# Softmax maxima of an attention kernel: split ahead of the turn, and the diagonal blocks' decay and maximum in one instruction

## The reference

```python
q, k, v = x @ W_q, x @ W_k, x @ W_v              # x is layer-normed
latent_kv = (k + v) @ W_down_kv
k_rec, v_rec = latent_kv @ W_up_k, latent_kv @ W_up_v   # 16 heads of 16
scores = einsum('bhqd,bhkd->bhqk', qh, k_rec) / math.sqrt(d)
scores = scores * exp(-0.01 * abs(t[:, None] - t[None, :]))
attn = softmax(scores)
out = (attn @ v_rec) @ W_o
x = x + out
```

## Time and profile before

| | |
|---|---|
| median of 3 runs | 6739.2 us (6736.05 to 6740.18) |
| profiled execution | 6737.1 us |
| its span on the core | 6735.3 us |
| PE busy | 5578.3 us (83%) |
| DVE busy | 4789.2 us (71%) |
| ACT busy | 3487.3 us (52%) |
| POOL busy | 2918.9 us (43%) |
| granted TensorE clock, mean | 0.919 |

### The profile page before, as it was taken

How to read it: one execution, slowest core, us unless ns; L and a number is a source line. 1 busy time by engine, 2 the same in 40 slices (tenths; PEclk the granted TensorE clock), 3 DMA queues, 4 the chain that set the end, 5 groups by cost and what they waited for, 6 DMA issues and landing times.

```text
span 6735.3 us, 109029 instructions
## 1 busy us (share of the span) xinstructions
PE 5578.3 (83%) x35596; PEld 3237.8 (48%) x35596; DVE 4789.2 (71%) x10653; ACT 3487.3 (52%) x5077; POOL 2918.9 (43%) x2244
## 2 busy tenths in 40 slices
PE   5489993688888889889888898898889975499992
PEld 5478882233433344334333443343434445388872
DVE  7655552677877878778778788787787867555674
ACT  1134442366666666666666666666666651144431
POOL 6700004455445454554555555545545117600166
PEclk9999996799999999999999999999999985599996
DMA  5433332333333333333333333333333225333486
GB/s 175 160 99 105 105 104 84 89 96 94 101 96 95 96 99 94 94 97 99 94 96 92 102 96 89 103 93 94 99 91 94 71 68 184 143 101 104 134 262 217
DMA packets 573334, 741.96 MB, mean 110 GB/s; under 512 B 104434, under 2 KB 490612, under 8 KB 572788
## 3 DMA queue, kind: packets, MB, share of 16 engines
q1 hardware_dynamic: 523636, 600.70, 30.4%
q0 software_dynamic: 49152, 134.28, 6.1%
HBM read 441.30 MB, written 293.34 MB: 109 GB/s over the span
## 4 chain that ended last, share of the span: by engine, by line
PE 57%; DVE 16%; POOL 15%; issue 7%; ACT 4%; DMA 1%; SPq 0%; POOLq 0%; DVEq 0%; ACTq 0%
PE psum L1059 11%; PE psum L346 10%; PE psum L948 9%; PE psum L958 7%; POOL xs L617 7%; PE psum L363 5%; DVE at_mx L1187 4%; DVE at_Sd L1183 2%; POOL at_qs L1267 2%; DVE at_mp L1208 2%; PE psum L961 2%; DVE at_mp L1210 2%; PE psum L1037 2%; DVE at_mab L1191 2%; PE psum L335 2%
## 5 line engine op out<-in xcount | busy, mean ns | idle before, releaser
L1187 DVE TENSOR_REDUCE at_mx<-psum 128x4 f32<-128x512 f32 x3584 | 2224.1, 681 | 704.3 <-PE psum L948 704.2
L1131 ACT ACTIVATE at_P<-psum 128x1024 f32<-128x1024 f32 x2048 | 2036.1, 1021 | 867.6 <-PE psum L961 865.7
L948 PE MATMUL psum<-at_kst,at_qst 96*128 96x128 bf16 (+3 forms) x7168 | 1350.7, 298 | 402.7 <-DVE at_mx L1187 384.5
L948 PEld LDWEIGHTS psum<-at_kst,at_qst 96*128 96x128 bf16 x7168 | 557.2, 99 | 1344.2 <-DVE at_mx L1187 844.8
L958 PE MATMUL psum<-at_qst,at_kst 99*128 99x512 bf16 (+3 forms) x5120 | 1153.3, 324 | 29.7 <-ACT at_P L1131 27.7
L1059 PE MATMUL psum<-at_P,at_V 128*17 128x512 f32 x8192 | 1125.1, 622 | 0.0
L1279 POOL TENSOR_TENSOR at_Sd<-at_Sd,at_m 128x1024 f32<-128x1024 f32 x256 | 484.7, 1906 | 527.3 <-DVE at_m L1201 524.0
L958 PEld LDWEIGHTS psum<-at_qst,at_kst 99*128 99x128 bf16 x5120 | 478.5, 100 | 311.9 <-ACT at_P L1131 49.0
L1230 POOL DMA_INDIRECT at_xT<-ys,at_yib x256 | 245.7, 960 | 790.8 <-DMA at_gab<-table 709.4
L961 PE MATMUL psum<-at_ident,at_Sd 128*128 128x128 f32 x2048 | 572.9, 280 | 0.0
L1258 POOL TENSOR_TENSOR at_OT<-at_On,at_rc 128x128 f32<-128x128 f32 x256 | 98.3, 405 | 1004.2 <-DVE at_rc L1215 1004.2
(11 more groups left out here) (248 smaller groups left out, 8214.2 us busy)
## 6 DMA issues: line engine op xcount, KB each, us to landing
parts<-at_pt SPq DMA_DIRECT2D x768, 128.0 KB
at_qst<-parts SPq DMA_DIRECT2D x1536, 64.0 KB, 2.3
at_kst<-parts SPq DMA_DIRECT2D x256, 192.0 KB, 3.0
m2X<-xs SPq DMA_DIRECT2D x272, 128.0 KB, 2.0
ys<-m2X SPq DMA_DIRECT2D x272, 128.0 KB
m1X<-xs SPq DMA_DIRECT2D x264, 128.0 KB, 2.0
ys<-m1X SPq DMA_DIRECT2D x264, 128.0 KB
at_kst<-parts SPq DMA_DIRECT2D x256, 128.0 KB, 2.9
```

Source lines behind the costliest of these rows:

```text
L948: ins = e.matmul(bank[(z + u) % 3][:, col - 512 * u:col - 512 * u + ln], self.qst[0:96, s, side, 128 * t:128 * t + 128], self.kst[0:96, s, ...
L1131: e.activation(self.P[:, i % NP, :], slot[a % 2], ACT.Exp).then_inc(self.taken.sem, 1)
L1187: e.tensor_reduce(self.mx[:, p % 2, hh, 8 * o + 4 * u:8 * o + 4 * u + 4], of, op=ALU.max, axis=AX.X).then_inc(self.s_read.sem, 1)
```

## The change

"mlo" and "fold" are gone from the plan. In the item "max", DVE now splits the maxima where they are, with queries on partitions: cast, subtract, cast, subtract on 128 x 16, into `mb` (128 x 3 x 16, bf16). PE turns all three parts with one bf16 matmul against a bf16 identity (48 rows out), after waiting for `m_parts`. ACT changes the sign in one copy of 48 x 128, and SP stores that, in another order of the DRAM tensor, so that each of the four loads reads rows of 1024 numbers. The diagonal blocks are read by `tensor_tensor_reduce`, one instruction for a block of 128 columns, which multiplies by `Dm`, writes `Sd` and gives the block's maximum.

```diff
--- before.py
+++ after.py
@@ -20,6 +20,7 @@
 E = 8
 B = 16
 LAM = 0.01
+LOWEST = -3.0e38
 EPS = 1e-5
 NBLK = 272
 XROWS = 16 * 128 * 89
@@ -675,7 +676,8 @@
         self.ve, self.sq, self.rs = sb("ve", [128, 8]), sb("sq", [128, 8]), sb("rs", [128, 8])
         self.mx, self.mab = sb("mx", [128, 2, 2, 56]), sb("mab", [128, 2, 16])
         self.m = sb("m", [128, 2, 16])
-        self.mT, self.mp = sb("mT", [16, 2, 128]), sb("mp", [16, 2, 3, 128], BF16)
+        self.mb, self.mr = sb("mb", [128, 2, 3, 16], BF16), sb("mr", [128, 16])
+        self.mp, self.identb = sb("mp", [48, 2, 128], BF16), sb("identb", [128, 128], BF16)
         self.yib, self.gab = sb("yib", [128, 8, 2], U32), sb("gab", [128, 8, 2])
         self.rows = self.xT[:].rearrange("p k (t d) -> p (k t) d", d=D)
         ctx.close()
@@ -698,6 +700,7 @@
         self.s_filled, self.s_read = sig.new("a_s_filled", 32 * NPAIR), sig.new("a_s_read", 32 * NPAIR)
         self.shifted = sig.new("a_shifted", 2 * NPAIR)
         self.m_max, self.m_parts = sig.new("a_m_max", NPAIR), sig.new("a_m_parts", NPAIR)
+        self.ident_cut = sig.new("a_ident_cut", 1)
         self.weighed, self.ou_copied, self.shared = sig.new("a_weighed", 8 * NPAIR), sig.new("a_ou_copied", NPAIR), sig.new("a_shared", NPAIR)
         self.spread, self.inverse = sig.new("a_spread", B), sig.new("a_inverse", NPAIR)
         self.summed = sig.new("a_summed", 4 * B)
@@ -708,7 +711,7 @@
         yield from (("weight", 0), ("weight", 1), ("weight", 2))
         yield from (i for f in (self.gather_order, self.prep_order) for i in f(0) if i)
         ahead = [i for b in range(1, B) for i in ((b, self.gather_order(b)), (b, self.prep_order(b)))]
-        late, after, split, fold = [], [], None, None
+        late, after, split = [], [], None
 
         def advance(queue):
             for item in queue[0][1]:
@@ -728,16 +731,10 @@
             score = (z // 8, self.ORDER[z % 8]) if z < 8 * NPAIR else None
             turn = (p, kb) if 0 <= s < 8 * NPAIR else None
             if split is not None:
-                yield from (("mlo", split), ("msend", split))
+                yield ("msend", split)
                 split = None
             if score or turn:
                 yield ("step", score, turn)
-            if fold is not None:
-                yield ("fold", fold, 1)
-                fold = None
-            if score and score[1] == self.DIAG:
-                yield ("fold", score[0], 0)
-                fold = score[0]
             if score and z % 8 == 7:
                 yield ("max", score[0])
                 yield ("sub", 2 * score[0] + 1)
@@ -911,13 +908,12 @@
             if kind == "msend":
                 p = at[0]
                 s, z = p % NS, p % 2
-                w.wait_ge(*self.m_parts.at(p + 1))
-                e.dma_start(self.mdram[z], self.mp[:, z]).then_inc(self.m_out.sem, 16)
+                w.wait_ge(*self.result("mturn", p))
+                e.dma_start(self.mdram[z].rearrange("c h t q -> (c h t) q"), self.mp[:, z]).then_inc(self.m_out.sem, 16)
                 w.wait_ge(*self.m_out.at(16 * (p + 1)))
                 for hh in (1, 0):
                     for v in range(2):
-                        e.dma_start(self.qst[96:99, 2 * s + hh, v, :].rearrange("c (t q) -> c t q", q=128),
-                                    self.mdram[z, 8 * hh:8 * hh + 8].rearrange("t c q -> c t q")).then_inc(self.m_rows[s].sem, 16)
+                        e.dma_start(self.qst[96:99, 2 * s + hh, v, :], self.mdram[z, :, hh].rearrange("c t q -> c (t q)")).then_inc(self.m_rows[s].sem, 16)
             if kind == "res":
                 b, t2 = at
                 w.wait_ge(*self.x1_out.at(16 * (b + 1)))
@@ -1013,8 +1009,9 @@
                 ins.then_inc(self.filled.sem, 1)
             if kind == "mturn":
                 p = at[0]
-                w.wait_ge(*self.m_max.at(p + 1))
-                e.transpose(to[0:16, 0:128], self.m[:, p % 2, :], self.ident[:]).then_inc(self.filled.sem, 1)
+                w.wait_ge(*self.m_parts.at(p + 1))
+                w.wait_ge(*self.ident_cut.at(1))
+                e.matmul(to[0:48, 0:128], self.mb[:, p % 2].rearrange("p c n -> p (c n)"), self.identb[:], start=True, stop=True).then_inc(self.filled.sem, 1)
             if kind == "norm":
                 p = at[0]
                 w.wait_ge(*self.ou_copied.at(p + 1))
@@ -1107,8 +1104,7 @@
             if kind == "mturn":
                 p = at[0]
                 w.wait_ge(*self.m_out.at(16 * (p - 1)))
-                e.activation(self.mp[:, p % 2, 0, :], of[0:16, 0:128], ACT.Copy, scale=-1.0)
-                e.activation(self.mT[:, p % 2, :], of[0:16, 0:128], ACT.Copy, scale=-1.0).then_inc(self.taken.sem, 1)
+                e.activation(self.mp[:, p % 2, :], of[0:48, 0:128], ACT.Copy, scale=-1.0).then_inc(self.taken.sem, 1)
             if kind == "norm":
                 p = at[0]
                 w.wait_ge(*self.shared.at(p - 1))
@@ -1145,6 +1141,7 @@
         w.wait_ge(*self.loaded.at(176))
         e.tensor_tensor(self.wk[:], self.wk[:], self.wv, ALU.add).then_inc(self.w_ready.sem, 1)
         e.tensor_scalar_mul(self.wq[:], self.wq[:], 1.0 / 16.0).then_inc(self.w_ready.sem, 1)
+        e.tensor_copy(self.identb[:], self.ident[:]).then_inc(self.ident_cut.sem, 1)
         last, z = None, 0
         for kind, *at in self.plan:
             if kind == "stats":
@@ -1180,34 +1177,31 @@
                         if o == self.DIAG:
                             if p >= 2:
                                 w.wait_ge(*self.full("T", p - 2, 7, hh))
-                            e.tensor_tensor(self.Sd[:, (2 * p + hh) % 4, 4 * u:4 * u + 4], of, self.Dm[:].rearrange("p (o k) -> p o k", o=1).to_broadcast([128, 4, 128]),
-                                            ALU.mult).then_inc(self.s_read.sem, 1)
+                            for t in range(4):
+                                ins = e.tensor_tensor_reduce(self.Sd[:, (2 * p + hh) % 4, 4 * u + t, :], of[:, t], self.Dm[:], 1.0, LOWEST, ALU.mult, ALU.max,
+                                                             accum_out=self.mab[:, 1, 8 * hh + 4 * u + t:8 * hh + 4 * u + t + 1])
+                            ins.then_inc(self.s_read.sem, 1)
                         else:
                             w.wait_ge(*self.m_max.at(p - 1))
                             e.tensor_reduce(self.mx[:, p % 2, hh, 8 * o + 4 * u:8 * o + 4 * u + 4], of, op=ALU.max, axis=AX.X).then_inc(self.s_read.sem, 1)
-            if kind == "fold":
-                p, hh = at
-                w.wait_ge(*self.s_read.at(32 * p + 4 * self.ORDER.index(self.DIAG) + 4))
-                last_fold = own.end(e.tensor_reduce(self.mab[:, 1, 8 * hh:8 * hh + 8], self.Sd[:, (2 * p + hh) % 4], op=ALU.max, axis=AX.X))
             if kind == "max":
                 p = at[0]
                 w.wait_ge(*self.s_read.at(z))
-                w.wait_ge(*last_fold)
                 k = own.end(e.tensor_reduce(self.mab[:, 0, :], self.mx[:, p % 2].rearrange("p h (t k) -> p (h t) k", k=7), op=ALU.max, axis=AX.X))
                 w.wait_ge(*k)
                 w.wait_ge(*self.shifted.at(2 * (p - 1)))
                 if p >= 2:
                     w.wait_ge(*self.full("mturn", p - 2))
                 e.tensor_tensor(self.m[:, p % 2, :], self.mab[:, 0, :], self.mab[:, 1, :], ALU.max).then_inc(self.m_max.sem, 1)
-            if kind == "mlo":
-                p = at[0]
-                mT, mp = self.mT[:, p % 2], self.mp[:, p % 2]
-                w.wait_ge(*self.result("mturn", p))
-                k = own.end(e.tensor_tensor(mT, mT, mp[:, 0], ALU.subtract))
-                w.wait_ge(*k)
-                k = own.end(e.tensor_copy(mp[:, 1], mT))
-                w.wait_ge(*k)
-                e.tensor_tensor(mp[:, 2], mT, mp[:, 1], ALU.subtract).then_inc(self.m_parts.sem, 1)
+                m, mb, mr = self.m[:, p % 2, :], self.mb[:, p % 2], self.mr[:]
+                w.wait_ge(*self.m_max.at(p + 1))
+                k = own.end(e.tensor_copy(mb[:, 0], m))
+                w.wait_ge(*k)
+                k = own.end(e.tensor_tensor(mr, m, mb[:, 0], ALU.subtract))
+                w.wait_ge(*k)
+                k = own.end(e.tensor_copy(mb[:, 1], mr))
+                w.wait_ge(*k)
+                e.tensor_tensor(mb[:, 2], mr, mb[:, 1], ALU.subtract).then_inc(self.m_parts.sem, 1)
             if kind == "share":
                 p = at[0]
                 w.wait_ge(*self.result("norm", p))
@@ -1314,7 +1308,7 @@
         xs = nc.dram_tensor("xs", [XROWS, D], F32).ap()
         ys = nc.dram_tensor("ys", [NBLK * 128, D], F32).ap()
         parts = nc.dram_tensor("parts", [2, 2, H, 3, HD, 2, S], BF16).ap()
-        mdram = nc.dram_tensor("mdram", [2, 16, 3, 128], BF16).ap()
+        mdram = nc.dram_tensor("mdram", [2, 3, 2, 8, 128], BF16).ap()
         tables = [nc.dram_tensor(f"table{i}", [128, NT, 2], dt).ap() for i, dt in enumerate((U32, F32))]
         we = {"rw": rw, "rb": rb, "g": eg, "u": eu, "d": ed}
```

## The result

The changed kernel takes 7084.5 us (median of 4 runs), 1.0514 times the kernel before on the same chip (95% interval 1.0495 to 1.0532), 346 us more. 7135 was forecast, 6850 to 7480 the range. The profiled execution's span is 7079.8 us.

What follows compares the result with a forecast made beforehand. In the attention PE's work sets the pace with no slack towards DVE, whose late first read moves the whole chain. 218 + 115 - 13 + 78 = +398 on 6737.1 gives 7135 us; range 6850 to 7480.

Steps and rivals of the forecast that it cites:

- The split: DVE's split of the maxima, moved ahead in each pair of heads: hole, clock, PE and ACT together +320 us.
- The blocks: Diagonal read in blocks of 0.30 us, two folds of 1.21 us removed: +0.6 us per pair, +78 us.
- The signs: Changed profile: casts, subtractions near 1.5 to 2 us, PE waits of 4 us, clean pair 32, clock below 0.93, blocks 0.3.
- the clock: PE in the attention, idling some 4.3 us in nearly every pair, loses clock: +0.9 us per pair, +115 us (0 to +166).
- The rhythm: Attention steps 2.98 us apart: DVE's first read, if late beyond its 0.5 us idle, moves scores, exponentials and weighted sum.
- The waits: Behind the maximum, one POOL operation comes between neighbouring split instructions; the last ends at 5.2 us, 4.4 to 6.1.
- the hole: Moved split ahead of DVE's next reads: 5.2 - 0.4 - 3.1 = +1.7 us per pair, +218 us (+115 to +333).
- PE, ACT and SP: One bf16 turn and one copy save 0.1 us per pair, -13 us; SP's earlier row loads gain 0.
- C: Rival: POOL does not get between the four split instructions, which end 0.85 us after the maximum; 6366 us; chance 0.09.
- B: Rival: in the diagonal each block instruction costs the full 0.45 us; 7445 us and above; chance of over 7480 is 0.07.
- E: Rival: the split stays as long, only elsewhere, a block costs 0.26 us, both parts cancel; 6737 us; chance 0.02.
- D: Rival: holes under 4 us leave the clock alone, blocks of 0.22 us; 6856 us, for 6755 to 6900; chance 0.08.

Runs made afterwards that it cites:

- the padded kernels: The one-line variant with one or three 1.21 us reductions over constant data directly behind the split: 6574.3 us (0.9733) and 7034.5 us (1.0415).
- one-line variant: The changed kernel, but POOL's two subtractions wait for the finished parts of the split instead of the maxima: 6462.3 us (0.9589).
- the split alone: The changed kernel with the diagonal blocks read and folded as before, the split still moved: 7092.9 us (1.0521).
- the blocks alone: The kernel before with the block instructions and no folds, the split where it was: 6717.1 us (0.9961).

## Why the prediction was right, and where it was off

- **The total**: the direction and the main mechanism were right, and the total is 51 us off, 7135 for 7084. That is closer than its parts, and partly luck. The split was forecast at +320 and alone measured +352. The blocks were forecast at +78 and measured -24 alone, and about -6 (346 - 352) in the changed kernel. One error of 32 and one of 84 have opposite signs.
- **The signs**: of those that the prediction names, the waits of PE (about once per pair, 4.1 us) and the clock (0.91) came. Of the instructions of the split the second cast and the first subtraction took 1.8 us, but the first cast took 0.175; a clean pair lasts 30.39 us, not 32; a block takes 0.21 us, not 0.3. And a bank of the diagonal takes 4 x 0.21 = 0.85 us, under the 1 us that the prediction calls a sign of being wrong. So its second part was wrong, as below.
- **The rhythm** (a late first read moves everything): shown, by the padded kernels. The row behind it was read wrongly: the 0.24 us in the earlier trace rows are not of a plain step. They lie in the step behind the maximum at 3098.53, whose two instructions had used up DVE's idle.
- **The waits** (one POOL operation between neighbours, the split ends at 4.4 to 6.1, middle 5.2): measured 5.17 in the mean, and 4.07 in the clean pair. There POOL's second subtraction ends at 3204.41, and the last instruction needs 0.17 behind the cast. POOL started beside the first cast, where the prediction had let it wait, so its low end was 0.3 too high. The one-line variant shows the cause.
- **The split's sum**: +218 for the hole, +115 for the clock, -13 for PE and ACT, 320 together; the split alone measured +352. The clock's term was about right there. The attention of the split alone has a mean clock of 0.92 over 4573 us, which takes 366 us from PE, against 211 at 0.95 over 4220. By the prediction's ratio of 2.3/3.3, which is from one pair, the 155 more are an estimate of 108. In the changed kernel 0.91 over 4564 us takes 411, and the 200 more are 139. That leaves 244 of the 352 for the hole and for PE and ACT, 39 more than the prediction's 205. The split's end was as forecast; the 3.1 us taken off has no run of its own, so where the 39 belong stays open.
- **PE, ACT and SP**: the gain on PE did not show. The bf16 turn takes 283 ns, the f32 one took 285; in the one-line variant, at a clock of 0.98, it takes 243. ACT's one copy takes 271 ns for two of 265 and 249. SP's part was near 0 as forecast: PE waited once, 0.9 us, for the rows of the maxima, and its weight load once, 1.8 us.
- **The blocks** were forecast to cost +78 us and gave -24 alone. Two things failed in that step. The start-to-start time is 0.21 us, the lower bound of 0.22 and not 0.30, because the accumulator read lies beside the next block; the prediction had put its 0.08 in the row. With 0.21 the step is 3.39. And the return to 2.98 behind it was wrong: that step has some 0.47 us of PE's own work, four f32 transposes of the sums (`norm`, 0.49 from their start at 3221.09 to the next scores), which the fold had covered. That puts the gain at 1.21 - 0.41 - 0.47 = 0.33 per pair, 42 us. The Trainium skill, VectorE: DVE Perf Modes, in its errata section, gives 120 cycles beside the columns, by which the prediction had estimated 258 ns a block and no change; the trace has 212 ns from start to start in a row (an entry by itself is 287 long), so for a row this was too high. Of the 42 us, 24 came in the kernel with the blocks alone. In the changed kernel at most 8 did, which is within the noise. The attention's clock was 0.94 with the blocks alone against 0.95 before, and 0.91 against 0.92 with the split, so the clock can have taken part of it back; no run separates this.
- **The rivals**: C, faster, would need the four to run without POOL between them. It does not hold in the changed kernel, but the one-line variant makes its condition true: the four end 0.84 us after the maximum. The time was 6462 for C's 6366. This is nearer than C's reasons allow: with the blocks at the measured -24 in place of its +78, C would give 6264, so its gain from the short hole is 198 us too large. Which term is at fault was not tested. B's and E's block prices, 0.45 and 0.26, were not met. D's was (0.21), but not its other half, a clock left alone.

## What to carry to other kernels

A small vector instruction is priced by what runs beside it: four dependent instructions of 0.17 us, 0.84 together, became 5.17 because the signal just ahead of them started the other engine's work in SBUF. One line that gives this signal later turned a kernel 5% slower than the one before into one 4% faster. Put short casts and two-input operations where the neighbour engine is held still, by letting it wait for the last of them, and let it run beside reads from PSUM. And where PE waits for the engine that has the hole, waits of some 4 us cost more than their length, since PE came back from them at half its clock.

## What the runs showed of the hardware that was not expected

- The accumulator read is an instruction of its own in the trace (0.083 us) that lies beside the next block in a row of block instructions: with it 0.212 us from start to start for 128 columns. A read of 512 columns takes 0.62 in a row.
- A reduction over one element does the work of a cast and did not wait for POOL in any of 256 cases: 171 ns at most, against 1810 in the mean for the cast at the same place.
- The hole's price is not proportional to its length. One pad of 1.2 us cost 0.76 to 0.88 us per pair at a mean clock of 0.96, two more, 2.4 us, cost 3.6 at 0.91.
- POOL's subtraction did not wait for a cast that had started 0.05 us ahead of it: 1895 ns in the mean in the changed kernel, and 1895 in the one-line variant, where no cast runs beside it. That is as far as the lengths show it.
